# A transformer block with a dense mixture of experts: one byte arena split into two typed arenas, with fewer and smaller staging buffers

## The reference

```python
q = x @ w_q                          # 16 heads of 128, rotary positions
k = (x @ w_kv_down) @ w_k_up         # 4 key/value heads, rotary positions
v = (x @ w_kv_down) @ w_v_up
mask = outside_window(512) & ~(key % 64 == 0) | future_block(128)
out = softmax(where(mask, -inf, q k / sqrt(128))) v @ w_o

probs = softmax(x @ gate.T); the 8 largest of 32, renormalised
# indices 5 to 8 move to the most similar of the first 4 where similarity >= 0.5
combine = sum of one_hot(index) * weight          # tokens x 32
for e in 32 experts:                              # dense: all tokens
    g, u = split(x @ gate_up[e].T)                # 2 x 768 columns
    y += (silu(g) * u) @ down[e].T * combine[:, e]
```

## Time and profile before

| | us |
|---|---|
| three runs: lowest, median, highest | 7145.95, 7717.48, 7742.63 |
| profiled execution | 7044.29 |
| its span, slowest core | 7042.8 |
| spans of the eight cores in it | 7023.4 to 7042.8 |
| granted TensorE clock, mean of each core | 0.832 to 0.837 of 2.4 GHz |

### The profile page before, as it was taken

How to read it: one execution, slowest core, us unless ns; L and a number is a source line. 1 busy time by engine, 2 the same in 40 slices (tenths; PEclk the granted TensorE clock), 3 DMA queues, 4 the chain that set the end, 5 groups by cost and what they waited for, 6 DMA issues and landing times.

```text
span 7042.8 us, 56361 instructions; the slowest of 8 cores (7023.4 to 7042.8 us)
## 1 busy us (share of the span) xinstructions
PE 5118.6 (73%) x20631; PEld 2145.2 (30%) x21044; DVE 2109.8 (30%) x3099; ACT 908.2 (13%) x1032; POOL 35.3 (1%) x69
## 2 busy tenths in 40 slices
PE   2544666400388888887888888887978798888888
PEld 0211112100133333333333333333333333333333
DVE  5443443455422222222222222222222222222222
ACT  1101331000001111010101011110101010111101
POOL 1000000000000000000000000000000000000000
PEclk6766668755689989898989899999989898998989
DMA  5111003100123333232323233332323232333324
GB/s 170 49 47 44 0 1 102 45 0 0 48 102 126 117 123 119 108 132 108 122 114 123 103 124 119 121 121 107 131 108 132 105 123 102 126 117 123 117 111 156
DMA packets 109004, 694.04 MB, mean 99 GB/s; under 512 B 12768, under 2 KB 12896, under 8 KB 54560
## 3 DMA queue, kind: packets, MB, share of 16 engines
q1 hardware_dynamic: 99440, 648.20, 25.2%
q0 software_dynamic: 9296, 42.21, 1.8%
HBM read 681.97 MB, written 8.39 MB: 98 GB/s over the span
## 4 chain that ended last, share of the span: by engine, by line
PE 70%; DVE 16%; issue 8%; ACT 3%; DMA 1%; DVEq 1%; ACTq 0%; POOL 0%; POOLq 0%; SPq 0%
PE P L1117 43%; PE P L1158 18%; DVE arena L1134 3%; DVE arena L1108 3%; PE P L648 2%; PE P L847 2%; DMA arena<-x_win 1%; PE P L787 1%; PE P L803 1%; ACT arena L749 1%; DVEq L158 1%; ACT arena L771 1%; PE P L480 1%; PE P L740 0%; DVE arena L1137 0%
## 5 line engine op out<-in xcount | busy, mean ns | idle before, releaser
L1117 PE MATMUL P<-arena 128*128 128x512 bf16 x12042 | 3045.8, 416 | 771.6 <-DVE arena L1108 752.7
L1117 PEld LDWEIGHTS P<-arena 128*128 128x128 bf16 x12288 | 1281.4, 105 | 2536.4 <-issue 1350.9
L1158 PE MATMUL P<-arena 128*128 128x512 bf16 x6020 | 1324.4, 379 | 10.5 <-DVE arena L1137 4.0
L1134 DVE TENSOR_TENSOR arena<-arena,P 128x1024 f32<-128x1024 f32 x192 | 234.5, 1221 | 2931.6 <-PE P L1117 2931.6
L1158 PEld LDWEIGHTS P<-arena 128*128 128x128 bf16 x6144 | 600.0, 98 | 732.5 <-issue 11.2
L1131 ACT ACTIVATE arena<-P 128x1024 f32<-128x1024 f32 x192 | 196.4, 1023 | 3395.6 <-PE P L1117 3395.6
L1166 DVE TENSOR_TENSOR arena<-arena,P 128x1024 f32<-128x1024 f32 x256 | 312.6, 1221 | 998.2 <-PE P L1158 998.2
L1145 ACT CAST arena<-arena 128x1536 bf16<-128x1536 f32 x256 | 375.0, 1471 | 909.1 <-PE P L1158 909.1
L1108 DVE CAST arena<-arena 128x2048 bf16<-128x2048 f32 x384 | 452.1, 1219 | 0.0
L648 PE MATMUL P<-arena 128*128 128x512 bf16 x502 | 142.5, 450 | 196.8 <-DVE arena L641 196.0
L1137 DVE TENSOR_TENSOR arena<-arena 128x1024 bf16<-128x1024 f32 x192 | 235.2, 1225 | 20.7 <-DVE arena L1134 0.9
(11 more groups left out here) (184 smaller groups left out, 1501.5 us busy)
## 6 DMA issues: line engine op xcount, KB each, us to landing
arena<-wg SPq DMA_DIRECT2D x384, 1024.0 KB, 6.2
arena<-wd SPq DMA_DIRECT2D x256, 768.0 KB, 4.6
arena<-x_win POOLq DMA_DIRECT2D x32, 768.0 KB, 5.3
arena<-wq SPq DMA_DIRECT2D x16, 1024.0 KB, 4.8
arena<-wo SPq DMA_DIRECT2D x16, 1024.0 KB, 4.9
arena<-x_win POOLq DMA_DIRECT2D x16, 512.0 KB, 21.8
out<-arena POOLq DMA_DIRECT2D x16, 512.0 KB, 6.6
arena<-wkv SPq DMA_DIRECT2D x4, 1024.0 KB, 12.7
```

The lines of the kernel that those rows point to most:

```text
L1117: mk.op("pe", lambda E, ps=ps, par=par, c=c, s2=s2: E.matmul(out=ps[:, s2 * 512:(s2 + 1) * 512], lhsT=wbf[par][:, c * 128:(c + 1) * 128], ...
L1134: mk.op("dve", lambda E, pu_=pu_, tpar=tpar: E.tensor_tensor(out=t2_sb[tpar], in0=t1_sb[tpar], in1=pu_[:, :], op=ALU.mult), reads=[b_t1s[t ...
L1158: first=(ei == 0 and j == 0): E.matmul(out=ps[:, s2 * 512:(s2 + 1) * 512], lhsT=wdbf[par][:, (ei * NDJ + j) * 128:(ei * NDJ + j + 1) * 128 ...
```

## The change

The byte arena becomes a float32 arena of 90112 bytes and a bfloat16 arena of 122624 bytes per partition; the views need no change of type any more. To fit in them, buffers are dropped and lifetimes moved:

- `wst` has one buffer in place of two, in all stages; the experts use a new single `wst2` of the same size. Every weight load so waits for the cast of the block just before it. `wbf` keeps two buffers (`wbf2` from the output projection on).
- `wdst` has one buffer of 768 columns in place of two of 1536: each down block comes as two loads of 384 KB and two casts.
- `xbfT`, `t1_sb`, `t2_sb` and `cbc_sb` have one buffer in place of two.
- The mask of 5120 columns is gone: the exponentials are multiplied by a column `pad01` (0 or 1 for a key block), and for `kk` up to 7 a 128-column piece by the triangular block `r4` in a second product. The ring has five slots in place of six.
- The queries `q` are allocated after the keys and values are done; the rotary temporaries have 1024 columns in place of 1536.

The diff, cut (the replacement of `wst[par]` by `wst` is the same in the key/value, query and output projections, and `sqt` has become a new buffer `sqt8` at its second use):

```diff
-        ART = st.enter_context(nc.sbuf_tensor("arena", [128, 212800], U8))
+        ARTF = st.enter_context(nc.sbuf_tensor("arena_f", [128, 22528], F32))
+        ARTB = st.enter_context(nc.sbuf_tensor("arena_b", [128, 61312], BF16))
...
-            v = self.t[:, off:off + cols * esz].bitcast(dt)
+            v = self.t[:, off // self.esz: off // self.esz + cols]
...
-        wst, b_wst = A.alloc("wst", 2048, F32, nbufs=2)
-        wbf, b_wbf = A.alloc("wbf", 2048, BF16, nbufs=2)
+        wst, b_wst = A.alloc("wst", 2048, F32)
+        wbf, b_wbf = A.alloc("wbf", 2048, BF16, nbufs=2, side="hi")
...
-        xbfT, b_xbfT = A.alloc("xbfT", WIN, BF16, nbufs=2, side="hi")
+        xbfT, b_xbfT = A.alloc("xbfT", WIN, BF16, side="hi")
...
-        PT_sb, b_ptv = A.alloc("pt", 4 * 6 * 640, BF16, side="hi")
+        PT_sb, b_ptv = A.alloc("pt", 4 * 5 * 640, BF16, side="hi")
...
-                        mk.op("dve", lambda E, hl=hl, slot=slot, kk=kk, W=W: E.tensor_tensor(
-                                out=PT_sb[:, hl * 3840 + slot * 640: hl * 3840 + slot * 640 + W],
-                                in0=PT_sb[:, hl * 3840 + slot * 640: hl * 3840 + slot * 640 + W],
-                                in1=mc_sb[:, MCOFF[kk]:MCOFF[kk] + W], op=ALU.mult),
-                              reads=[pts, b_mc], writes=[pts])
+                        mk.op("dve", lambda E, hl=hl, slot=slot, kk=kk, W=W: E.tensor_scalar(
+                                out=PT_sb[:, hl * 3200 + slot * 640: hl * 3200 + slot * 640 + W],
+                                in0=PT_sb[:, hl * 3200 + slot * 640: hl * 3200 + slot * 640 + W],
+                                scalar1=pad01_sb[:, kk:kk + 1], scalar2=None, op0=ALU.mult),
+                              reads=[pts, b_p01], writes=[pts])
+                        if kk <= 7:
+                            r0off = (kk - max(kk - 4, 0)) * 128
+                            mk.op("dve", lambda E, hl=hl, slot=slot, r0off=r0off: E.tensor_tensor(
+                                    out=PT_sb[:, hl * 3200 + slot * 640 + r0off: hl * 3200 + slot * 640 + r0off + 128],
+                                    in0=PT_sb[:, hl * 3200 + slot * 640 + r0off: hl * 3200 + slot * 640 + r0off + 128],
+                                    in1=r4_sb, op=ALU.mult),
+                                  reads=[pts, b_r4], writes=[pts])
...
-        wdst, b_wdst = A.alloc("wdst", 1536, F32, nbufs=2, side="hi")
+        wst2, b_wst2 = A.alloc("wst2", 2048, F32)
+        wdst, b_wdst = A.alloc("wdst", 768, F32, side="hi")
...
-        t1_sb, b_t1s = A.alloc("t1sb", NTQ, F32, nbufs=2, side="hi")
-        t2_sb, b_t2s = A.alloc("t2sb", NTQ, F32, nbufs=2, side="hi")
-        cbc_sb, b_cbc = A.alloc("cbcsb", NTQ, F32, nbufs=2, side="hi")
+        t1_sb, b_t1s = A.alloc("t1sb", NTQ, F32, side="hi")
+        t2_sb, b_t2s = A.alloc("t2sb", NTQ, F32, side="hi")
+        cbc_sb, b_cbc = A.alloc("cbcsb", NTQ, F32, side="hi")
...
-                    mk.op("sp", lambda E, e=e, j=j, par=par: E.dma_start(out=wst[par], in_=wg_h[e, j]),
-                          writes=[b_wst[par]], dma=True)
-                    mk.op("dve", lambda E, par=par: E.tensor_copy(out=wbf[par], in_=wst[par]),
-                          reads=[b_wst[par]], writes=[b_wbf[par]])
+                    mk.op("sp", lambda E, e=e, j=j, par=par: E.dma_start(out=wst2, in_=wg_h[e, j]),
+                          writes=[b_wst2], dma=True)
+                    mk.op("dve", lambda E, par=par: E.tensor_copy(out=wbf2[par], in_=wst2),
+                          reads=[b_wst2], writes=[b_wbf2[par]])
...
-                mk.op("sp", lambda E, grp=grp, m=m, par=par: E.dma_start(out=wdst[par], in_=wd_h[grp, m]),
-                      writes=[b_wdst[par]], dma=True)
-                mk.op("act", lambda E, par=par: E.copy(out=wdbf[par], in_=wdst[par]),
-                      reads=[b_wdst[par]], writes=[b_wdbf[par]])
+                for hf in range(2):
+                    mk.op("sp", lambda E, grp=grp, m=m, hf=hf: E.dma_start(
+                            out=wdst, in_=wd_h[grp, m][:, hf * 768:(hf + 1) * 768]),
+                          writes=[b_wdst], dma=True)
+                    mk.op("act", lambda E, par=par, hf=hf: E.copy(
+                            out=wdbf[par][:, hf * 768:(hf + 1) * 768], in_=wdst),
+                          reads=[b_wdst], writes=[b_wdbf[par]])
```

More of the change, by code:

```diff
@@ L293, in build_nc, with _trunc @@
+        A = DualArena()
         bP = [mk.buf(f"P{i}", excl=True) for i in range(4)]
         bOut = [mk.buf(f"out{c}") for c in range(NCD)]
-        def _trunc(phase):
+        def _trunc(phase, store=None):
             if UPTO != phase:
                 return False
[L299 to L303, removed]
+            if store is not None:
+                acc_v, accb = store
+                for c in range(NCD):
+                    mk.op("pool", lambda E, c=c: E.dma_start(out=out_h[c * 128:(c + 1) * 128, :],
+                                                             in_=acc_v[:, c * NTQ:(c + 1) * NTQ]),
+                          reads=[accb[c]], writes=[bOut[c]], dma=True)
+            else:
+                dmy, b_dmy = A.alloc("dmy", 1024, F32)
+                mk.op("dve", lambda E: E.memset(dmy, 0.0), writes=[b_dmy])
+                for c in range(NCD):
+                    mk.op("pool", lambda E, c=c: E.dma_start(out=out_h[c * 128:(c + 1) * 128, :], in_=dmy),
+                          reads=[b_dmy], writes=[bOut[c]], dma=True)
@@ L360, in build_nc @@
                   writes=[b_xst[par]], dma=True)
[L361 to L365, removed]
+            mk.op("dve", lambda E, par=par: E.tensor_copy(out=xbfT, in_=xst[par]),
+                  reads=[b_xst[par]], writes=[b_xbfT])
+            mk.op("act", lambda E, par=par: E.square(out=sqt[par], in_=xbfT),
+                  reads=[b_xbfT], writes=[b_sqt[par]])
+            for i, (src, bsrc, pbase) in enumerate([(xbfT, b_xbfT, 0), (sqt[par], b_sqt[par], 2)]):
                 for s3 in range(3):
@@ L782, in build_nc @@
                         kb = LT + r
-                        slot = kb % 6
+                        slot = kb % 5
                         off = (LT - max(kb - 4, 0)) * 128
-                        ap_cols = [(hl * 3840 + slot * 640 + off) for hl in range(4)]
+                        ap_cols = [(hl * 3200 + slot * 640 + off) for hl in range(4)]
                         pt_reads.extend(b_pts[hl][slot] for hl in range(4))
```

166 lines of the change are left out of this document (89 added, 77 removed).

## The result

| us | before | changed |
|---|---|---|
| median of ten runs each | 7646.84 | 7991.59 |
| lowest, highest | 7044.91, 7791.52 | 7839.61, 8257.96 |
| profiled execution | 7044.29 | 7847.93 |

The changed kernel takes 1.113 times as long (95% interval 1.111 to 1.116) over the executions in which no die of the chip shows a lowered PE clock; in the others one die or both do, which makes them up to 11% longer before and up to 5% longer after, so that the medians differ by 4.5% only (and two executions of the experiments' kernels, one in experiment 5 and one in experiment 8, took 17588 and 20848 us, with cores at clocks down to 0.29).

A forecast was written before the change was run, and what follows sets the result against it. The PE was taken to bound the kernel, through gate/up and down matmuls; the change would make down weight staging pace the down steps. Profiled 7044 + 957 (down weights) + 35 (clock) + 7 (first stage) = 8043 us, range 7750 to 8560.

The forecast's parts named there:

- if it is PE time, the down stage would swallow its share: Median's extra 673 us: if PE time, the load-paced down stage absorbs 30%, so such runs end near 8510.
- The main term: Down weights: two half loads and casts through one buffer make a step 9.2 us against the PE's 5.18, +957 us.
- 480h - 1250: Down stages: total loss in us over 16 groups, h being the time of one half load and cast, 4.6 us.
- The clock behind it: Down stage's last steps and the next group's first matmuls, changed by the PE clock after pauses: +35 us.
- Gate/up weights at 0: Expert gate/up stage: the single 1 MB buffer's up load, usable 6.4 us later, is covered by the gate block's matmuls.
- up weights come late too: Rival, gate/up stage: loads of 9 us cost 1.1 us in each of 192 pairs, +211, 8254 us; chance 0.04.
- t1, t2, cbc at 0, attention at 0: Experts' single product buffers cost 0; attention's column mask products and five slots 0, bounds 0 to 42 us for the products.
- First stage at +7: First stage: with one xbfT the cast period goes from 3.9 to 4.3 us, +7 us, bounds 0 and 15.
- The load's fixed part is smaller: Rival, down loads: a 384 KB load takes 2.8 us, h = 4.0, +670, 7756 us; chance 0.12.
- The load hardly shrinks: Rival, down loads: 384 KB takes 3.9 to 4.3 us, +1198 to +1390, 8284 to 8476 us; chance 0.12.
- The PE's clock sets the down step: Rival, down steps: at clock 0.5, 24 matmuls take 10.0 us, over 9.2: +192, 8235 us; chance 0.08.
- Not slower: Rival, down loads: half loads scale as pure bandwidth and faster, L at most 1.7 us, total within 2%; chance 0.04.

The follow-up runs named there:

- experiment 5: Changed kernel with two down staging buffers of 768 columns, viewed in the bfloat16 arena, in place of one: 7103.9 us on the slowest core, cores 0 to 3 at 7020 to 7031.
- experiment 8: Changed kernel with two down half buffers, DVE's next casts moved ahead and combine weights behind an expert's first pair: 5990.2 us, 104 over the same order in the kernel before.
- experiment 4: Kernel before with two down staging buffers of 768 columns, one per half, in place of two of 1536: 7023 to 7030 us on cores 4 to 7.
- experiment 6: Kernel before with one down staging buffer of 384 columns, four 192 KB loads and four casts a step: 9096.7 us, cores from 8902 to 9095.
- experiment 2: Kernel before with one wst, t1, t2, cbc and xbfT each, down buffers kept: 7082.2 us, six of eight cores at 7027 to 7047.

## Why the prediction was wrong

**What it was compared with.** The mechanism and its sign were right, but the forecast of 8043 is +4.2% on the 7717 that stands as the time before, and the like-for-like change is +11.3%. The step that failed is the last of the sum: it was made on the profiled execution, 7044 (+14.2%), and then left beside a median 673 us higher, of which the text said that "no row says where". Within the sum the term that was mis-sized is the down weights', +957 where +788 was measured (next paragraph), which puts 8043 at 195 us over the profiled 7848. The forecast should have been told as a change of each: +1000 for an execution like the profiled one, and for one like the median 7717 to 8510, +10%. The measured medians moved from 7647 to 7992, less than that: half of the ten runs after lie within 2% of the lowest, and the longest is 418 us over it, where before the longest was 747 over. That the median after lies 51 us from 8043 is luck, since the sum was made for an execution like the profiled one.

The traces say where such time goes. In experiment 4 cores 0 and 1, with 1800 us at a granted clock of 0.812, took 227 us longer in the gate/up stages than cores 4 to 7 and 58 us longer in the down stages (1394 against 1336), and the same up to the experts. So it is PE time, and the down stages' share is a fifth, not 30%. In experiment 6, where the down steps wait for loads, the four cores with that level took 124 us longer in the gate/up stages and 7 in the down stages. So the step "if it is PE time, the down stage would swallow its share" holds.

**The main term: mechanism right, size 190 us too high.** Put at +957, the down stages measured +788. Its terms:

| term of a half, us | forecast | measured |
|---|---|---|
| cast's end to issue | 0.07 | 0.08 |
| load L | 3.4 | 3.1 |
| landing to cast | 0.3 | 0.13 |
| cast | 0.8 | 0.83 |
| h, mean of all halves | 4.6 | 4.20 to 4.25 |

With h = 4.20 to 4.25 the formula 480h - 1250 gives 766 to 790, so the form of the sum (step 0 free, step 1 late by less, the chain behind) holds. The formula itself was slightly off: it kept step 0's second half at 4040.1 whatever h is, and with that moving too it is 496h - 1325, the same at 4.6 and 758 to 783 here. Step 1 then starts 2.3 to 2.5 us late, not 3.5; core 1 has 2.0 to 3.0.

Two terms were mis-sized. The load: the two slopes that I averaged, 0.75 and 1.08 us for 384 KB, are both too flat for this step. Loads alone on the queue take 2.4, 3.1, 4.4 and 4.8 to 5.0 us at 192, 384, 768 and 1024 KB. From 384 to 768 KB that is 1.3 us. From 768 to 1024 KB it is some 0.5 us, as the rows before said; the mistake was to carry this slope down to half the size. The second slope came from the engines' busy time, which is not latency. The gate load that spoke for 4.3 us at 256 KB was a poor witness: in the same execution its time on the eight cores goes from 2.6 to 4.3 us, with a median of 3.0, and in the changed kernel from 2.5 to 2.9. The Trainium skill has a fit for a software-issued load (DMA: Bandwidth & Descriptors, Anatomy of one DMA), 2.0 us plus bytes over 436 GB/s. By estimate from it the four loads, which SP issues on the hardware queue, would take 2.45, 2.9, 3.8 and 4.4 us: right for the smallest, up to 0.6 us short for the others, and the measurement decides. Landing to start: I carried 0.3 us from DVE after a load issued by POOL to ACT after a load issued by SP. There it is 0.13 us in the median of 496 casts.

**The clock behind it.** Put at +35 for the last step and the next group's first matmuls, and right. The last steps take 6.25 us in the mean (core 1) where they took 5.34, 15 us over 16 groups, and a group's first 32 matmuls 8.4 to 8.5 us where they took 7.2, 19 us over 15. The gate/up stages as a whole grew by 8 us only. Inside the stage the half clock shows as forecast, in somewhat less than every other step, and is hidden.

**Gate/up weights at 0.** Right: idle 767.7 against 771.6, and experiment 2. (Experiment 8 shows what else the single buffer does once the pauses are gone.) The rival "up weights come late too" falls.

**t1, t2, cbc at 0, attention at 0.** Right as far as the totals can tell: the attention's score matmuls run from 713.3 to 1114.6 us, 401 us, against 710.9 to 1111.8, 401 us; the 192 column multiplications take 58.4 us and the 128 small products 28.8, covered.

**First stage at +7.** The last cast starts 66.3 us after the first (before: 12.7 to 76.8, 64.1): +2. The row that the period was read from is right where the PE is at half clock, 4.33 us; at the upper level the matmuls take 0.81 instead of 1.44 us and the period is 3.7. The cast's own view, its first and last start, and whom it waited for (us, times):

```profile
L389 DVE CAST arena_b<-arena_f x16: 959/960/961, 14.0 to 80.3; 128x1536 bf16<-128x1536 f32 x16
...
  PE P L401: 46.9, 14
```

**The other rivals.** "The load's fixed part is smaller" (L 2.8, 7756) is nearer to the profiled 7848 than the forecast is, which lies below the forecast's own 7900 to 8240: L came out at 3.1, on the edge between the two, and landing to start at less than half of its 0.3. "The load hardly shrinks" falls by experiment 6. "The PE's clock sets the down step" falls: steps of 7.03 us end some 1.2 us before the next weights come, and only the rare ones of 8.2 us leave little or none. "Not slower" needed L of 1.7 us; even 192 KB take 2.4.

## What to carry to other kernels

A single staging buffer costs when wait, load latency, landing and cast add up to more than the work that one filling feeds: 6.4 us against 7 to 9 us of matmuls was free, 4.2 us twice against 5.18 was 50 us a group. Even where it feeds its own matmuls in time it can hold up the loads behind it in the same queue, as the 104 us of experiment 8 show. If memory is short, split a buffer into two halves used in turn rather than keep one whole or one half: the same 1536 columns gave about 7030 us as two halves and 7260 to 7334 as one. And before buffers, look at the order of the engine that feeds the PE: moving the next casts ahead (one before the pair's two products, one right behind them, two before the down steps) together with the combine weights was worth 16%. What each of these moves is worth alone was not tried.

## What the runs showed of the hardware

- The latency of a load from memory, issued by SP and alone on its queue: 2.4 us at 192 KB, 3.1 at 384, 4.4 at 768, 4.8 to 5.0 at 1024. Four times 192 KB in a row so takes 9.6 us, one times 768 KB 4.4. Every load has 128 rows, one for each partition, so the rows shrink with the load; size and row length were not separated.
- From landing to the start of the waiting instruction: 0.13 us for ACT after a load issued by SP, where DVE took 0.3 us after one issued by POOL (0.1 for the first two). DVE after a load issued by SP takes 0.09 us (192 up casts of the changed kernel), so the waiting engine does not make the difference.
- Where loads set the pace, long and short steps tend to alternate. Pauses of 2.86 and 3.11 us were followed by steps of 7.03 us, which leave pauses of 1.22 and 1.03 us, and these by steps of 5.34 us. Of 568 steps behind a pause of 1 to 2 us 560 took 5.34 us. It isn't the last pause alone: of 607 steps behind one of 2.75 to 3.25 us 151 ran at the upper level, like this one near a group's end.
- Besides 0.5 and 1.0 the traces have a third granted clock, 0.812. It shows on pairs of cores or on a whole die, for up to 1800 us of one execution (experiment 4), and on no core in the profiled executions of the kernel before and of the changed one.

```profile
4466.37 5.34 PE L1206 MATMUL P<-arena_b 128*128 128x512 bf16 x24 [3.15 <-ACT arena_b L1192]
```
